# Two attention layers and two feed-forwards on one core: layer 1's queries multiplied by their scales ahead of their turn, inverse roots beside the centring, and the first scores directly behind the second feed-forward product

## What is computed

```python
x = x + xattn0(layernorm(x), ctx)   # 16 heads of 64, ctx 375 rows
x = x + ffn0(layernorm(x))          # rows quantised to int8, ternary weights, depthwise conv of 3, silu
x = x + xattn1(layernorm(x), ctx)   # 16 heads of 16, with
    q = rms_norm(q, q_norm_w);  k = rms_norm(k, k_norm_w)      # x * rsqrt(mean(x*x) + 1e-6) * w, by head
    q = apply_rope(q, ...);     k = apply_rope(k, ...)
    out = softmax(q k^T * D**-0.5) v @ Wo.T
x = x + ffn1(layernorm(x))          # uint8 activations, int8 weights
```

## Time and profile before

| | us |
|---|---|
| runs | 2429.35, 2430.49, 2436.9 |
| median | 2430.49 |
| the profiled execution | 2424.58 |
| its span, first to last instruction | 2422.8 |
| busy: PE, weight loads, DVE, POOL, ACT | 2332.0, 1764.1, 1658.7, 1646.3, 1570.3 |

### The profile page before, as it was taken

The page is one execution under the profiler, slowest core; times in us unless marked ns, Lnnn a source line. Parts: engine busy times, 40 slices in busy tenths (PEclk is TensorE's granted clock), DMA queues, the critical chain, the costliest instruction groups (busy, mean ns, idle before and its releaser), DMA issues.

```text
span 2422.8 us, 61267 instructions
## 1 busy us (share of the span) xinstructions
PE 2332.0 (96%) x20064; PEld 1764.1 (73%) x20064; DVE 1658.7 (68%) x4412; ACT 1570.3 (65%) x4305; POOL 1646.3 (68%) x1894
## 2 busy tenths in 40 slices
PE   6999999999999999999999999999999999999578
PEld 5777777777777777777777777777777777777336
DVE  6666666776666677666666766666677666666785
ACT  4666666766666676666666766666676666767346
POOL 3766777666668767666776666677667667776507
PEclk9999999999999999999999999999999999999789
DMA  4000000000000000000000000000000000000202
GB/s 161 27 11 10 10 8 10 2 10 10 10 10 8 10 2 10 10 10 10 10 8 5 7 10 10 10 10 8 10 2 10 10 10 10 8 4 0 56 10 62
DMA packets 31197, 37.04 MB, mean 15 GB/s; under 512 B 3284, under 2 KB 29636, under 8 KB 31172
## 3 DMA queue, kind: packets, MB, share of 16 engines
q1 hardware_dynamic: 31172, 36.71, 5.2%
HBM read 29.36 MB, written 7.34 MB: 15 GB/s over the span
## 4 chain that ended last, share of the span: by engine, by line
PE 85%; ACT 5%; DVE 5%; issue 3%; POOL 2%; DMA 0%; ACTq 0%; POOLq 0%; DVEq 0%; SPq 0%
PE ps L339 25%; PE ps L400 15%; PE pt L424 10%; PE pa L436 5%; PE ps L383 5%; PE pa L471 5%; PE pa L451 4%; PE pt L414 4%; ACT prob L790 3%; PE pt L339 2%; PE pa L339 2%; DVE nmx L1025 1%; PE pa L605 1%; PE pa L563 1%; ACT q L830 1%
## 5 line engine op out<-in xcount | busy, mean ns | idle before, releaser
L1025 DVE TENSOR_REDUCE nmx<-ps 112x2 f32<-112x750 f32 x512 | 476.2, 935 | 183.9 <-PE ps L400 177.7
L1462 POOL TENSOR_TENSOR prob<-prob,rinv 112x375 f32<-112x375 f32 x512 | 405.0, 812 | 259.9 <-DVE rinv L1041 256.2
L1462 POOL TENSOR_TENSOR f1w_room<-f1w_room,rinv 112x375 f32<-112x375 f32 x512 | 404.7, 814 | 26.2 <-DVE rinv L1041 22.4
L746 ACT ACTIVATE room<-ps 128x375 f32<-128x375 f32 (+2 forms) x480 | 227.5, 487 | 267.6 <-PE ps L339 267.6
L746 ACT ACTIVATE probT<-pt 125x336 f32<-125x336 f32 (+1 forms) x512 | 242.5, 474 | 138.0 <-PE pt L414 84.1
L1487 POOL TENSOR_TENSOR krs<-krs,nhalf 125x48 f32<-125x48 f32 x32 | 257.1, 8033 | 0.0
L400 PE MATMUL ps<-kT,q 64*112 64x375 f32 x1024 | 227.9, 521 | 11.4 <-ACT prob L790 10.2
L1016 DVE COPY probT<-pt 125x336 f32<-125x336 f32 x322 | 161.8, 502 | 95.9 <-PE pt L424 95.9
L400 PE MATMUL ps<-room,q 64*112 64x375 f32 x1024 | 220.8, 512 | 3.0 <-ACT prob L790 1.9
L790 ACT ACTIVATE prob<-ps,nmx 112x375 f32<-112x375 f32 x256 | 144.7, 576 | 70.2 <-DVE nmx L1025 70.2
L436 PE MATMUL pa<-probT,room 125*64 125x112 f32 x3072 | 182.5, 264 | 0.0
(11 more groups left out here) (267 smaller groups left out, 5579.7 us busy)
## 6 DMA issues: line engine op xcount, KB each, us to landing
craw<-in_ctx SPq DMA_DIRECT2D x32, 375.0 KB, 3.1
xin<-in_x SPq DMA_DIRECT2D x32, 112.0 KB, 2.0
x_rows<-x SPq DMA_DIRECT2D x32, 112.0 KB, 1.9
out<-probT SPq DMA_DIRECT2D x16, 224.0 KB, 2.4
room<-x_rows SPq DMA_DIRECT2D x1, 2576.0 KB, 13.3
stage<-in_f1w SPq DMA_DIRECT2D x2, 1024.0 KB, 5.1
stage<-in_wk SPq DMA_DIRECT2D x1, 1024.0 KB, 6.9
stage<-in_wv SPq DMA_DIRECT2D x1, 1024.0 KB, 9.3
```

Of the source, the lines that this page charges most:

```text
L746: return act.activation(dst, src, ACT.Copy)
L1025: top = dve.tensor_reduce(nmx[:, g:g + 2], ps[0:T, 2 * (i % 2):2 * (i % 2) + 2, 0:S], AX_X, ALU.max, negate=True)
L1462: pool.tensor_tensor(prob(i, n), prob(i, n), rinv[:, g:g + 1].to_broadcast([T, S]), ALU.mult).then_inc(s["normed"], 1)
```

## The change

Five parts, with the line numbers of the changed program in its rows.

1. Centring without the root. For x1, DVE subtracts the mean (`centre`), takes the largest absolute value, and only then waits for POOL's root: the root multiplies the maximum, and root and 127 / maximum together make the factor of the rounding. For x2, the centred rows go to the query product as they are, and the root is multiplied in later, in the rotary instructions and the squares.
2. Queries scaled ahead of their turn. `query_squares` follows the rotary sum at once; POOL does two roots of eight heads each before pair 1; DVE multiplies each half of the queries by its heads' scales (`query_scale`), and `query_turn(b, c)` transposes each half apart, the first behind value piece 5, the second behind turn 2. Both go to bank 1 of `pa`. Maxima and exponentials of layer 1 take no scale.
3. ACT's order: the query copies come one pair later, behind exponential 5, and the copy of value piece 4 behind exponential 1.
4. PE's order: scores 0 directly behind the second feed-forward product, then value piece 3 and the transposes of x2, then the remaining query heads. `row_sum(0)` comes ahead of the rotary instructions.
5. In the first feed-forward the quantised row's transposes stand half a key piece earlier, four value terms instead of two stand behind the input's transposes, and DVE normalises the next input before it waits for the hidden products.

The diff, cut to its core:

```diff
@@ pe: attention and query_turn @@
+            def query_turn(b, c):
+                pe.wait_ge(s["q1_norm"], b * DC + (c + 1))
+                pe.transpose(pa[:, 1, c * T:(c + 1) * T], q1b[:, c * P:(c + 1) * P], ident[0:T, 0:T])\
+                    .then_inc(s["q1T_ready"], 1)
...
+                    if part == MIDDLE and pair_of(i + AHEAD, part) == (1, 0):
+                        pe.wait_ge(s["q1_sb"], b + 1)
...
                     if part == MIDDLE and i == 0:
-                        query_turn(b)
+                        pe.wait_ge(s["q1_rope"], b + 1)
                         pe.wait_ge(s["q1_sq"], b + 1)
                         v0_proj(b + 1, [5])
+                        query_turn(b, 0)
...
+                    if part == MIDDLE and i == 3:
+                        query_turn(b, 1)
@@ pe: rest @@
-                    k0_proj(b + 1, range(1, 5), True)
+                    k0_proj(b + 1, range(1, 4), True)
+                    pe.wait_ge(s["k0_sb"], b * IC + (IC + 1))
+                    k0_terms(4, 0, 3)
...
-                    k0_terms(5, 0, 3)
+                    k0_terms(4, 3).then_inc(s["k0_ready"], 1)
...
-                    k0_proj(b + 1, [6, 7], True)
+                    k0_proj(b + 1, [5, 6, 7], True)
...
-                    v0_terms(2, 0, 4)
+                    v0_terms(2, 0, 2)
...
                 if not last_batch:
+                    pe.wait_ge(s["q0_sb"], b * 2 + 3)
+                    scores(0, MIDDLE, b)
                     v0_proj(b + 1, [3])
@@ act @@
-                    scale = 1.0 if layer == 0 else qrs[:, 2, h:h + 1]
...
-                        if part == MIDDLE and i == 2:
+                        if part == MIDDLE and i == 3:
                             query_copies(b)
...
-                act.activation(qsq, pa[0:T, 0, 0:D], ACT.Square).then_inc(s["q1_sq"], 1)
+                act.wait_ge(s["q1_read"], b + 1)
+                act.activation(qsq, pa[0:T, 0, 0:D], ACT.Square, scale=st[:, 2, 2:3]).then_inc(s["q1_sq"], 1)
@@ dve @@
+            def query_scale(b, c):
+                dve.wait_ge(s["q1_rope"], b + 1)
+                dve.wait_ge(s["q1_rstd"], b * DC + (c + 1))
+                half = q1b[:, c * P:(c + 1) * P].rearrange("p (h e) -> p h e", e=DH1)
+                dve.tensor_tensor(half, half, qrs[:, 2, 8 * c:8 * c + 8].unsqueeze(2).to_broadcast([T, 8, DH1]),
+                                  ALU.mult).then_inc(s["q1_norm"], 1)
...
+                link(dve.tensor_reduce(am[:, 0:1], src, AX_X, ALU.max, apply_absolute_value=True))
+                dve.wait_ge(s["rstd1"], b + 1)
+                link(dve.tensor_scalar(am[:, 0:1], am[:, 0:1], st[:, 1, 2:3], A8_EPS, ALU.mult, ALU.max))
+                link(dve.reciprocal(am[:, 1:2], am[:, 0:1]))
+                link(dve.tensor_scalar(am[:, 1:2], am[:, 1:2], st[:, 1, 2:3], 127.0, ALU.mult, ALU.mult))
...
+                dve.wait_ge(s["q1_read"], b + 1)
+                dve.scalar_tensor_tensor(q1b[:], xr[:], st[:, 2, 2:3], q1b[:], ALU.mult, ALU.add)\
+                    .then_inc(s["q1_rope"], 1)
+                query_squares(b)
+                if not last_batch:
                     row_max(1, MIDDLE, b)
                 else:
+                    for c in range(DC):
+                        query_scale(b, c)
                     query_masks(b)
@@ pool @@
+                def query_root(c):
+                    heads = slice(8 * c, 8 * c + 8)
+                    pool.tensor_tensor(qrs[:, 2, heads], qrs[:, 1, heads], nhalf[0:T, 0:8], ALU.pow)\
+                        .then_inc(s["q1_rstd"], 1)
+
+                if not last_batch:
+                    attention(part, b, 0, 1)
                 pool.wait_ge(s["q1_var"], b + 1)
...
+                query_root(0)
+                query_root(1)
+                attention(part, b, 0 if last_batch else 1, PAIRS if last_batch else G)
```

More of the change, by code:

```diff
@@ L599, in rest @@
                 if not last_batch:
-                    pe.wait_ge(s["q0_sb"], b * 2 + 3)
-                    scores(0, MIDDLE, b)
+                    q0_proj(b + 1, 1, range(1, HT))
                 pe.wait_ge(s["k1T_sb"], b * DC + DC)
@@ L781, in exps @@
                 act.wait_ge(s["maxed"], at(i + 1, part, b))
-                if layer == 1 and p % 2 == 0:
-                    act.wait_ge(s["q1_rstd"], b * 4 + (p // 2 + 1))
                 if part != OPENING or i >= 4:
@@ L1026, in row_max @@
                                         negate=True)
-                if layer == 1:
-                    link(top)
-                    if p % 2 == 0:
-                        dve.wait_ge(s["q1_rstd"], b * 4 + (p // 2 + 1))
-                    for n in range(2):
-                        h = HEADS1[2 * p + n]
-                        top = dve.tensor_scalar(nmx[:, g + n:g + n + 1], nmx[:, g + n:g + n + 1], qrs[:, 2, h:h + 1],
-                                                None, ALU.mult)
                 top.then_inc(s["maxed"], 1)
@@ L1116, in attention @@
                     if part == MIDDLE and i == 0:
[L1117 removed]
+                        query_masks(b)
                     if i >= 1:
                         turned(i - 1, part, b)
+                    if part == MIDDLE and i == 1:
+                        query_scale(b, 1)
                 if part != CLOSING:
```

101 lines of the change are left out of this document (35 added, 66 removed), and 2 rows, old and new, of the table names.

## The result

The changed kernel takes 2391.82 us (2388.96 to 2393.14, 4 runs) against 2431.01 us (2429.35 to 2436.9, 4 runs) of the kernel before: a ratio of 0.984, 95% interval 0.9824 to 0.9856. That is faster, as forecast, and inside the range of 2390 to 2428, but the gain is 39 us and not 17. Between the two profiled executions the gain is 33.2 us. The forecast had 17.

The account below looks back on a forecast made before the run. TensorE, 96% busy but with waits in three places, bounds the kernel; -0.27 + 0.48 - 0.77 = -0.56 us a batch, times 31 is 17 us, median 2413 us; own range 2405 to 2422, 8 in 10 2390 to 2428.

Parts of the forecast that it names:

- Wait ahead of the query product: TensorE before each batch's first layer 0 query product: two value-term pairs moved behind the input's transposes remove the wait, -0.27 us.
- the early row: First norm's quantised row, centred beside GpSimd's inverse root: about 0.65 us sooner, wanted 0.53 sooner; gain 0, at worst 0.1 lost.
- The start chain: Layer 0 queries, from rotary sum held under GpSimd's multiply through exponential 1 to pair 5's score product: that product +0.9 us.
- From scores 5 to turn 4: Pairs 5 to 7: query copies behind exponential 5 remove a 0.5 us wait; delay falls from +0.9 to +0.48, transposes 4 add 0.
- Layer 1: Eight head pairs 4 to 11 without scalings or scale column: TensorE waits less, -0.77 us in a batch.
- The 0.25 each for turns 6 and 8: Probability transposes of pairs 6 and 8: second half no longer waits behind VectorE's maximum and two scalings, 0.25 us each.
- The 0.09 for each of three score products: Score products ahead of transposes 6 and behind transposes 7 and 9: 0.09 us sooner each, between 0 and 0.35.
- Rival 1: Rotary sum slips in before GpSimd's multiply or isn't held: all behind 0.6 to 0.7 us sooner, 37 us, 2393; chance 0.26.
- Rival 2: GpSimd's roots hold VectorE's multiply of the queries' first half, 1.4 us later: +0.85 a batch, 2457 us; chance 0.08.
- Rival 3: No measurable change: layer 1 waits are pipeline gaps, or opening pairs lose 0.5 more; 2424 to 2430 us, chance 0.16.
- The last batch: Final batch: copies wait for both roots (+3.4 us), norms (1.5) and eight pairs (about 2) shorter; 0, within 1.5.

## Why the prediction came out as it did

- **Wait ahead of the query product** (-0.27): right in size at the product (-0.28), -0.18 at the end of the second feed-forward, whose product takes 0.97 us from start to start now that a score product follows it, and not 0.79. The size was luck, the credit went to the wrong part: with the order undone and the early row kept, the product is 0.04 us late, so 0.24 of the 0.28 are the early row's, which the forecast had at 0. At the end of the second feed-forward the order has 0.11 of the 0.18.
- **The start chain is the step that failed**: "1220.4 + 4.6 + 0.5 = 1225.5 for scores 5, +0.9". Measured +0.10. In the changed kernel its place and mechanism stand (exp 1 alone 0.30 later costs 0.27, a copy behind it 0.47); its terms were too large one by one, all in the same direction. Counted from the end of the feed-forward, the rotary sum ended 0.33 us sooner than forecast (it began 0.05 sooner and took 0.92, not 0.7 of hold and 0.5 of its own), reduction and variance took 0.54 for 0.65, and exp 1 came at 8.22 us where the forecast had 8.73 and before had 8.36. From exp 1 to scores 5 the forecast had 5.1, a 4.6 of before plus the whole copy; it was 4.82, because the 4.6 held waits that the copy filled; the rows below show them. 0.51 + 0.28 = 0.79, of the 0.8 that were missed. What is left of the delay is PE's own order, which is why scores 3 come 0.11 later too.
- **From scores 5 to turn 4** (0.42 less): 0.37, right in size; that the wait on exp 5 is gone the traces show, but of what took it away only 0.10 us is shown.
- **Layer 1** (-0.77): -0.65. The 0.25 each for turns 6 and 8 were right (0.28: the values follow after 0.80 and 0.81 us, and after 1.09 and 1.08 before). The 0.09 for each of three score products were nothing: from scores 8 to turn 6 it is 2.30 us in both traces, to turns 8 and 10 2.31 before and 2.29 and 2.30 now.
- **Rivals.** Rival 1 had the time almost right (2393) by a cause that did not occur: the sum was held, and freeing it gained nothing. That the time fits it is luck. Rival 2 fell with line 1052. Rival 3 fell with turns 6 and 8. The forecast's own range, 2405 to 2422, was too narrow, since an error of 0.3 us in one term of a chain is 9 us, and three such errors shared a sign. The last batch (0 within 1.5) and the feed-forward behind the loop, from that batch's first value product (L436) to the end, took 182.8 us after and 182.9 before.

ACT's row from exp 1 to scores 5, maximum 3 first, then exp 3's first exponential, its last read and scores 5. Before (exp 1 at 1220.03, scores 5 at 1224.62):

```profile
1222.28 0.93 DVE L1025 TENSOR_REDUCE nmx<-ps 112x2 f32<-112x750 f32 x1
...
1223.24 0.57 ACT L790 ACTIVATE f1w_room<-ps,nmx 112x375 f32<-112x375 f32 x1
...
1224.26 0.20 ACT L790 ACTIVATION_READ_ACCUMULATOR f1w_room<-ps,nmx 112x1 f32 x1
```

In the changed kernel (exp 1 at 1203.02, scores 5 at 1207.84):

```profile
1206.52 0.62 ACT L790 ACTIVATE f1w_room<-ps,nmx 112x375 f32<-112x375 f32 x1
...
1207.52 0.26 ACT L790 ACTIVATION_READ_ACCUMULATOR f1w_room<-ps,nmx 112x1 f32 x1
```

Before, exp 3 waited for maximum 3 (until 1223.21), 0.50 us behind the start of ACT's copy of turn 0; now it follows that copy after 0.33. So 0.17 of the new copy went into that wait. Scores 5 came 1224.62 - 1224.46 = 0.16 us behind ACT before and come 1207.84 - 1207.78 = 0.06 behind it now: another 0.10. So in the kernel before scores 5 was not waiting for ACT, as the forecast read it: it followed PE's own row (0.70 us behind the start of turn 1, the least in any of these runs), and the first 0.1 us of a later ACT cost nothing.

The Trainium skill, "SBUF — State Buffer", section "Who interferes with whom", has the later of two such instructions block until the other ends. The trace agrees for multiplies (0.923 us against 0.484 with one input in PSUM). It does not agree for the roots, which read SBUF too: under them DVE's multiply with two SBUF inputs took at most 0.293 us.

## What to carry to other kernels

A span between two events of the trace contains waits: before a new instruction is added to it, take the waits out, since the instruction fills them first. Where several engines' rows of work end at the same product, shortening one shows nothing (three edits here gave 0 each) and is no proof that it has room for more; try the cut of all of them together (-0.27). An undoing must rebuild the operand forms too: a factor from a constant in place of a column hid 60% of a term. And read off the trace how much later an inserted instruction really makes things: one of 0.41 us delayed exp 1 by 0.30, which is the difference between 0.14 us of room and none.

## What the runs showed of the hardware

- A DVE multiply or sum with two SBUF inputs is held under a GpSimd multiply (0.44 us here), the same instruction with one input in PSUM is not, and under GpSimd's powers the multiply is not held (at most 0.293 us). After the release the sum took 0.28 of its 0.48 us, and the multiply 0.15 of its 0.28.
- GpSimd's power costs by the column: 1.65 us for 8 columns of 112 rows, as worked out from 1.02 for 4 and 8.03 for 48.
- A column in place of a constant as factor costs DVE 0.06 us on a 112x1 instruction and ACT 0.09 us on an exponential of 375 columns.
- A pair of TensorE products of 512 columns takes 0.47 us among its like. Behind the query product it takes 0.65, and 0.75 if a score product comes next.
